# Attention scores computed as 512 cached and 64 new keys instead of two halves of 288

## The chip, the cores and the metric

The kernel runs on one core of a Trainium2 chip. The metric is the device time of one execution in microseconds (us); lower is better. Engines are called as the profile calls them: PE is TensorE's matmul side, PEld its weight loads, DVE is VectorE, ACT is ScalarE, POOL is GpSimd, SP is SyncE, which here only issues DMAs.

## The reference

The layer is a cross attention over a context of 1601 rows, a grouped-query attention and a gated feed-forward part, each added to x of 8 x 64 tokens by 512 features. The part that matters here is the second:

```python
k_sel = k_cache[block_idx].reshape(-1, NKV, HD)      # 16 blocks of 32 = 512 cached keys
k_full = jnp.concatenate([k_sel, k[0]], axis=0)      # + 64 new keys = 576
qh = q.transpose(0, 2, 1, 3)
scores = jnp.einsum('bhld,bhtd->bhlt', qh, k_full) / math.sqrt(HD)
attn = jax.nn.softmax(scores, axis=-1)
out = jnp.einsum('bhlt,bhtd->bhld', attn, v_full)
```

There are 32 query heads and 8 key heads (so 4 query heads share the keys of one group g), a head has 128 features, and there are 512 query tokens. Each head thus needs 512 x 576 scores.

## The kernel before

The program runs three stages one after the other on all engines: the cross attention (to about 290 us of the span), the grouped-query attention, called the head stage here (about 292 to 757 us), and the feed-forward part (to the end). Only the head stage is touched.

**Tiles of the head stage.** A head n (0 to 31) is the i-th of four in group g. Its 512 query tokens are four tiles qt of 128. For each tile, `score` (L1514) makes 128 x 576 scores in PSUM; DVE takes the negated row maximum (L1889), ACT the exponential with that bias and the row's sum (L1756), DVE inverts the sum (L1872), POOL scales the probabilities (L2015), PE turns them (`turn_probs`, L1540 and L1549) and multiplies them with the values (`mix`, L1558 to L1567). PE also computes the next head's queries (`queries`, L1509) and, once per group, the output projection (`output`, L1582, 48 products).

**Precision.** Every product of the stage other than the turns is made of three passes over numbers split in a high and a low part, both in the format fp32r (a 32-bit float of reduced mantissa): high x high, high x low, low x high, all added up in one PSUM bank. One matmul instruction loads 128 x 128 weights (here: the query tile, `q_t`) and then streams the moving operand (here: the keys) column by column. Each of the six products of a score tile loads its own weights, since the program issues a load for every product.

**PSUM.** A bank holds 512 numbers of 32 bits per partition. A tile of 576 scores needs two banks: 0 and 1 for even qt, 2 and 3 for odd qt. Before, each holds a half of 288 keys:

```python
for half in range(2):
    bank = 2 * (qt % 2) + half
    keys = bass.ds(g * KEYS + half * HALF, HALF)
    for step, (a, b) in enumerate(PASSES):
        mm = pe.matmul(psum[:, bank, 0:HALF], q_t[a][:, qt * P:(qt + 1) * P],
                       (k_high, k_low)[b][:, keys], start=(step == 0), stop=(step == 2))
```

**What sets the order.** It is written out by hand: `head` on PE works on qt = 0 to 3 and does, for each, a part of the next head's queries, the turn of the head before (`turn_probs`) and the score tile of this head; after the fourth come the rest of the queries and `mix` of the head before. A score tile waits until ACT has read the tile two before it (semaphore `exp`), since there are two pairs of banks. DVE and ACT wait for the last of the six products (semaphore `s`). The first DMAs of the feed-forward weights (L323) are issued by SP when the last score tile of head 31 is done. In head 30, bank 3 also holds a small sum in columns 288 to 290, which DVE reads (L1886).

Of the kernel before, what the change touches and what calls it, by code (L numbers as in the profile page):

```python
# [17 lines left out]
ALU = mybir.AluOpType  # L18
ACT = mybir.ActivationFunctionType
AX = mybir.AxisListType  # L20

P = 128
# [3 lines left out]
BATCH, SEQ, DIM = 8, 64, 512  # L26
# [25 lines left out]
NSEL = TOPK * BLOCK  # L52
ST = NSEL // P
KEYS = NSEL + SEQ

HALF = KEYS // 2
# [14 lines left out]
def wait(eng, sem, count):  # L71

    if isinstance(count, int) and count <= 0:
        return
    eng.wait_ge(sem, count)
# [1283 lines left out]
def turn_bank(qt):  # L1359

    return 4 + qt % 2


def attention_and_ffn(core, own, qo, first, xh, xl, k_high, k_low, v_sel, v_new, free):


    nc, arg, psum = core.nc, core.arg, core.psum
# [3 lines left out]
    wq_nat, wq_t, q_t = qo["wq"], qo["wq_t"], qo["q_t"]  # L1371
    wo_t = core.pack(free["wo_t"], *((f"wo_t_{s}", [P, REP, DIM], F32R) for s in ("high", "low")))
    value_high = core.sb("value_high", [P, ST + 1, HD], F32R, ctx=own)
    value_low, probs, turned_high, turned_low, mixed_high, mixed_low, piece2 = core.pack(
        free["rest"], ("value_low", [P, ST + 1, HD], F32R), ("head_probs", [P, TT, KEYS], F32),
        ("probs_t_high", [P, ST + 1, TOK], F32R), ("probs_t_low", [P, ST, TOK], F32R),
        ("mixed_t_high", [P, REP, TOK], F32R), ("mixed_t_low", [P, REP, TOK], F32R), ("w_piece2", [P, 2, PIECE], F32))
    value, probs_t, mixed_t = [value_high, value_low], [turned_high, turned_low], [mixed_high, mixed_low]
    neg_max = core.sb("neg_max", [P, TT], ctx=own)
    den = core.sb("den", [P, TT], ctx=own)  # L1380
# [8 lines left out]
    s = {k: core.sem(v, own) for k, v in names.items()}  # L1389
# [21 lines left out]
    part = core.sb("abs_part", [P, 3], ctx=own)  # L1411
# [32 lines left out]
    def gate_bank(c, k):  # L1444
        return 4 + 2 * (c % 2) + k

    def last_bank(qt):

        return (4, 5, 2, 3)[qt]

    def has_weight(g, i):

        return not isinstance(g, int) or REP * g + i < NH - 2
# [11 lines left out]
    with nc.Block() as block:  # L1465
# [37 lines left out]
        def _(pe):  # L1503
# [9 lines left out]

            def score(g, n, qt):  # L1514

                wait(pe, s["exp"], TT * n + qt - 1)
                if qt == 0:
                    pe.wait_ge(s["ql"], n + 1)
                if isinstance(g, int) and n == NH - 2 and qt == 1:
                    pe.wait_ge(s_tot, NKV)  # L1520
                    pe.matmul(psum[:, 3, HALF:HALF + 3], ones[:, :], total[:, :], start=True, stop=True).then_inc(s_all, 1)
                elif isinstance(g, int) and n == NH - 2 and qt == 3:
                    pe.wait_ge(s_co, 1)
                for half in range(2):
                    bank = 2 * (qt % 2) + half
                    keys = bass.ds(g * KEYS + half * HALF, HALF)
                    for step, (a, b) in enumerate(PASSES):
                        mm = pe.matmul(psum[:, bank, 0:HALF], q_t[a][:, qt * P:(qt + 1) * P],  # L1528
                                       (k_high, k_low)[b][:, keys], start=(step == 0), stop=(step == 2))
                mm.then_inc(s["s"], 1)  # L1530

# [171 lines left out]
        def _(act):  # L1703
# [48 lines left out]
            def exponential(n, qt):  # L1752

                act.wait_ge(s["max"], TT * n + qt + 1)
                wait(act, s["pt"], TT * (n - 1) + qt + 1)
                act.activation(probs[:, qt, :].rearrange("p (a k) -> p a k", a=2),  # L1756
                               psum[:, 2 * (qt % 2):2 * (qt % 2) + 2, 0:HALF],
                               ACT.Exp, bias=neg_max[:, qt:qt + 1], accum_out=den[:, qt:qt + 1]).then_inc(s["exp"], 1)

            def turned_high(g, i, qt):  # L1760
                act.wait_ge(s["pt"], TT * (REP * g + i - 1) + qt + 1)
# [73 lines left out]
        def _(dve):  # L1835


            def query_weight_low(g, i):
                dve.wait_ge(s["wqh"], REP * g + i + 1)
                dve.tensor_tensor(flat_wq(1), wq_nat[:, i, :], flat_wq(0), ALU.subtract).then_inc(s["wql"], 1)  # L1840

            def queries_low(i, n):
                dve.wait_ge(s["qh"], n + 1)
                dve.tensor_tensor(q_t[1][:, :], psum[:, head_bank(i), :], q_t[0][:, :], ALU.subtract).then_inc(s["ql"], 1)
# [9 lines left out]
            def mixed_low(i, n):  # L1854

                dve.wait_ge(s["ah"], n)
                dve.tensor_tensor(mixed_t[1][:, (i - 1) % REP, :], psum[:, head_bank(i), :],
                                  mixed_t[0][:, (i - 1) % REP, :], ALU.subtract).then_inc(s["al"], 1)
# [4 lines left out]
            def turned_low(g, i, qt):  # L1863
                dve.wait_ge(s["th"], TT * (REP * g + i - 1) + qt + 1)
                dve.tensor_tensor(probs_t[1][:, 0:ST, qt * P:(qt + 1) * P],  # L1865
                                  psum[:, turn_bank(qt), :].rearrange("p (t q) -> p t q", t=ST),
                                  probs_t[0][:, 0:ST, qt * P:(qt + 1) * P], ALU.subtract).then_inc(s["tl"], 1)

            def invert(n, qt):
                dve.wait_ge(s["exp"], TT * n + qt + 1)  # L1870
                wait(dve, s["norm"], TT * (n - 1) + qt + 1)
                dve.reciprocal(rden[:, qt:qt + 1], den[:, qt:qt + 1]).then_inc(s["rd"], 1)  # L1872

            def output_weight_low(g, i):
                dve.wait_ge(s["woh"], REP * g + i + 1)
                dve.tensor_tensor(wo_t[1][:, i, :], wo_nat[:, i, :], wo_t[0][:, i, :],
                                  ALU.subtract).then_inc(s["wol"], 1)

            def head(g, i, this, last, nxt):
                n = REP * g + i  # L1880
                for qt in range(TT):
                    if this:
                        dve.wait_ge(s["s"], TT * n + qt + 1)
                        if isinstance(g, int) and n == NH - 2 and qt == 1:
                            dve.wait_ge(s_all, 1)
                            dve.tensor_scalar(coeff[:, :], psum[:, 3, HALF:HALF + 3], 1.0 / WSIZE, None,  # L1886
                                              ALU.mult).then_inc(s_co, 1)
                        wait(dve, s["exp"], TT * (n - 1) + qt + 1)
                        dve.tensor_reduce(neg_max[:, qt:qt + 1],  # L1889
                                          psum[:, 2 * (qt % 2):2 * (qt % 2) + 2, 0:HALF],  # L1890
                                          AX.XY, ALU.max, negate=True).then_inc(s["max"], 1)


                    if qt > 0 and this:
                        invert(n, qt - 1)
                    if qt == TT - 1 and last:
                        tail_low(i, n)
                    elif last:
                        turned_low(g, i, qt)
                if last:  # L1900
                    turned_low(g, i, TT - 1)
                if this:
                    invert(n, TT - 1)
                if nxt:
                    queries_low(i + 1, n + 1)
                if nxt and has_weight(g, i):
                    query_weight_low(g + (i + 2) // REP, (i + 2) % REP)
                if this and i > 0:
                    if i == 1:
                        output_weight_low(g, 0)  # L1910
                    output_weight_low(g, i)
                early_weights(g, i)
                if last:
                    mixed_low(i, n)
                if this and i == 0:
                    values_low(g)
                if i == 0 and last:
                    for qt in range(TT):
                        add_output(g, qt, turn_bank(qt))

            def tail_low(i, n):

                dve.wait_ge(s["tailh"], n)
                dve.tensor_tensor(probs_t[0][SEQ:P, ST, :], psum[0:SEQ, head_bank(i), :], probs_t[0][0:SEQ, ST, :],
                                  ALU.subtract).then_inc(s["taill"], 1)

            def add_output(g, qt, bank):
                dve.wait_ge(s["o"], TT * (g - 1) + qt + 1)
                dve.tensor_tensor(core.x[:, qt, :], psum[:, bank, :],  # L1929
                                  core.x[:, qt, :], ALU.add).then_inc(s["xo"], 1)  # L1930

            def early_weights(g, i):

                if not isinstance(g, int):
                    return
                if (g, i) == (NKV - 1, 2):
                    quantise(0, 0)
                    quantise(0, 1)
                elif (g, i) == (NKV - 1, REP - 1):
                    quantise(0, 2)  # L1940
                    low(0, 0)
                    low(0, 1)
# [223 lines left out]
```

## Time and profile before

| | us |
|---|---|
| median of 3 runs | 888.73 (888.36 to 892.6) |
| the profiled execution, its own time | 887.68 |
| its span | 885.7 |
| PE busy | 845.7 (95%) |
| PEld busy | 636.2 (72%) |
| DVE busy | 609.1 (69%) |
| ACT busy | 514.3 (58%) |
| POOL busy | 459.1 (52%) |

Busy time is that in which the engine had an instruction running. The time of one matmul in the rows is from its start to its modelled end, which is longer than the distance at which the next can follow; where matmuls stand in a row, the distance between two starts is what one costs. "Idle before" and an arrow name what ended an idle time.

### The profile page before, as it was taken

To read this page: it belongs to the slowest core of one execution; us is meant where nothing else is said; L and a number is where in the kernel's file an instruction comes from. 1 tells how busy PE (TensorE), PEld (TensorE's weight loads), DVE (VectorE), ACT (ScalarE), POOL (GpSimd) and SP (SyncE) were. 2 spreads that over 40 slices of the span, in tenths; PEclk is the share of its full clock that TensorE was granted. 3 is DMA by queue.
4 is the path that set the end of the run, shared out by engine and by line. 5 is a ranking of instruction groups with operands and counts; after the bars stand their busy time and mean duration, and the time that the engine had idled before them with its cause. 6 is when DMAs were issued, how large, how long until landed. Compare 5 with 4: busy or idle time off the path is not lost.

```text
span 885.7 us, 15315 instructions
## 1 busy us (share of the span) xinstructions
PE 845.7 (95%) x5246; PEld 636.2 (72%) x5246; DVE 609.1 (69%) x1002; ACT 514.3 (58%) x989; POOL 459.1 (52%) x294
## 2 busy tenths in 40 slices
PE   6899999999999599999999999999999998899998
PEld 4444555454534488888888888888888887788886
DVE  4755677567647377586775876758758589588773
ACT  4755646464656366565665656656656577455551
POOL 2598798887661343545435444454454543334430
PEclk9899999999999899999999999999999999999999
DMA  9553443204620333060240501505105005255621
GB/s 365 196 207 122 158 176 119 84 7 117 230 107 1 131 117 122 1 214 24 72 164 0 213 24 40 193 4 205 32 5 209 13 1 180 106 174 186 210 71 48
DMA packets 42338, 102.94 MB, mean 116 GB/s; under 512 B 7859, under 2 KB 12979, under 8 KB 41395
## 3 DMA queue, kind: packets, MB, share of 16 engines
q1 hardware_dynamic: 42002, 102.06, 33.0%
q8 instruction: 29, 0.48, 0.2%
q10 hardware_dynamic: 288, 0.26, 0.1%
q14 instruction: 19, 0.15, 0.1%
HBM read 96.95 MB, written 1.05 MB: 111 GB/s over the span
## 4 chain that ended last, share of the span: by engine, by line
PE 61%; DVE 2%; POOL 1%; DMA 1%; SPq 1%; ACT 0%; issue 0%; POOLq 0%; DVEq 0%
PE psum L1528 11%; PE psum L1509 9%; PE psum L1644 9%; PE psum L1582 9%; PE psum L1540 6%; PE psum L1658 4%; PE psum L1567 3%; PE psum L1558 3%; PE psum L1563 3%; PE psum L1549 1%; DMA ffn_raw<-in_L_ffn_mean_w_dram 1%; PE psum L1559 1%; PE psum L1561 1%; SPq L323 1%; POOL head_probs L2015 0%; POOL ffn_raw L2035 0%
## 5 line engine op out<-in xcount | busy, mean ns | idle before, releaser
L2015 POOL TENSOR_TENSOR head_probs<-head_probs,inverse_den 128x576 f32<-128x576 f32 x128 | 147.5, 1153 | 203.3 <-DVE inverse_den L1872 203.3
L1201 DVE TENSOR_REDUCE max_part<-psum 128x1 f32<-128x804 f32 x128 | 121.2, 990 | 50.6 <-PE psum L753 50.2
L1065 ACT ACTIVATE probs<-psum 128x512 f32<-128x512 f32 (+1 forms) x208 | 106.8, 608 | 57.5 <-PE psum L775 56.9
L1756 ACT ACTIVATE head_probs<-psum,neg_max 128x576 f32<-128x576 f32 x128 | 94.7, 740 | 54.2 <-DVE neg_max L1889 53.5
L1889 DVE TENSOR_REDUCE neg_max<-psum 128x1 f32<-128x576 f32 x128 | 96.9, 757 | 23.3 <-PE psum L1528 22.0
L623 POOL TENSOR_TENSOR prob_sums<-prob_sums,probs 128x1024 f32<-128x1024 f32 (+1 forms) x42 | 100.2, 2385 | 7.2 <-ACT probs L1065 2.7
L1528 PE MATMUL psum<-k_high,query_t_high 128*128 (+1 forms) x256 | 87.1, 340 | 2.8 <-POOL value_low L2044 2.8
L623 POOL TENSOR_TENSOR prob_sums<-probs 128x1024 f32<-128x1024 f32 x30 | 71.3, 2381 | 33.0 <-ACT probs L1065 32.9
L1540 PE MATMUL psum<-ident,head_probs 128*128 128x128 f32 x496 | 78.9, 275 | 7.8 <-POOL head_probs L2015 6.5
L1865 DVE TENSOR_TENSOR probs_t_low<-psum,probs_t_high 128x512 fp32r<-128x512 f32 x124 | 84.7, 683 | 1.0
L2035 POOL TENSOR_TENSOR ffn_quant<-ffn_raw 128x1536 f32<-128x1536 f32 x13 | 45.6, 3512 | 68.5 <-DVE ffn_w_low L1951 26.9
L775 PE MATMUL psum<-q_t,c_t 97*128 97x512 f32 (+1 forms) x208 | 75.7, 436 | 5.4 <-ACT probs L1065 4.2
L753 PE MATMUL psum<-c_t,q_t 96*128 96x402 f32 x256 | 74.8, 375 | 4.7 <-DVE max_part L1201 4.1
L1762 ACT ACTIVATE probs_t_high<-psum 128x512 fp32r<-128x512 f32 x124 | 73.0, 588 | 6.1 <-PE psum L1549 6.1
L1528 PE MATMUL psum<-k_high,query_t_low 128*128 (+1 forms) x256 | 76.5, 299 | 0.0
L1528 PE MATMUL psum<-k_low,query_t_high 128*128 (+1 forms) x256 | 76.4, 298 | 0.0
L1540 PEld LDWEIGHTS psum<-ident,head_probs 128*128 128x128 f32 x496 | 61.4, 141 | 17.6 <-issue 10.4
L753 PEld LDWEIGHTS psum<-c_t,q_t 96*128 96x128 f32 x256 | 42.6, 188 | 42.5 <-DVE max_part L1201 28.4
L775 PEld LDWEIGHTS psum<-q_t,c_t 97*128 97x128 f32 (+1 forms) x208 | 37.1, 186 | 32.4 <-ACT probs L1065 26.9
L2027 POOL TENSOR_TENSOR w_piece<-w_piece 128x1024 f32<-128x1024 f32 x21 | 49.9, 2404 | 9.0 <-DVE value_low L1851 9.0
L1929 DVE TENSOR_TENSOR x<-psum,x 128x512 f32<-128x512 f32 x32 | 22.1, 690 | 46.9 <-PE psum L1582 46.9
L1528 PEld LDWEIGHTS psum<-k_high,query_t_high 128*128 128x128 f32 x256 | 49.3, 193 | 3.5 <-POOL value_low L2044 3.2
(242 smaller groups left out, 1903.3 us busy)
## 6 DMA issues: line engine op xcount, KB each, us to landing
ctx_t_odd<-in_ctx_dram SPq DMA_DIRECT2D x4, 3202.0 KB, 10.7
ffn_raw<-in_L_ffn_w_dram SPq DMA_DIRECT2D x42, 256.0 KB, 3.9
ffn_raw<-in_L_ffn_mean_w_dram SPq DMA_DIRECT2D x42, 256.0 KB, 4.2
w_piece<-in_L_ffn_w_dram SPq DMA_DIRECT2D x21, 512.0 KB, 6.5
w_piece<-in_L_ffn_mean_w_dram SPq DMA_DIRECT2D x21, 512.0 KB, 7.8
cache<-in_ctx_dram SPq DMA_DIRECT2D x3, 3202.0 KB, 10.5
wq_nat<-in_L_attn_wq_dram SPq DMA_DIRECT2D x32, 256.0 KB, 7.4
wo_nat<-in_L_attn_wo_dram SPq DMA_DIRECT2D x32, 256.0 KB, 3.2
```

Source lines behind the costliest of these rows:

```text
L623: pool.tensor_tensor(total[rows, :], (prob_buffer(b, t - 1) if first else total)[rows, :], prob_buffer(b, t)[rows, :], ALU.add).then_inc(s ...
L753: mm = pe.matmul(psum[:, bank + k, 0:PIECE_KEYS], q_t[0:SHIFT, b, 2 * qt:2 * qt + 2, :].rearrange("p h n -> p (h n)"), c_t[0:SHIFT, b % 3, ...
L775: pe.matmul(psum[0:rows_of(t), n % SCORE_BANKS, :], lhs, rhs[:, half * BANK:(half + 1) * BANK], start=True, stop=True).then_inc(s_sb, 1)
L1065: act.activation(prob_buffer(b, t)[0:rows, half * BANK:(half + 1) * BANK], psum[0:rows, n % SCORE_BANKS, :], ACT.Exp, scale=XSCALE).then_i ...
L1201: dve.tensor_reduce(max_part[:, qt, pair:pair + 1], psum[:, bank:bank + 2, 0:PIECE_KEYS], AX.XY, ALU.max).then_inc(s_max, 1)
L1509: mm = pe.matmul(psum[:, head_bank(i), :], wq_t[a][:, c, :], (xh, xl)[b][:, c, :], start=(k == 0), stop=(k == 3 * DC - 1))
L1528: mm = pe.matmul(psum[:, bank, 0:HALF], q_t[a][:, qt * P:(qt + 1) * P], (k_high, k_low)[b][:, keys], start=(step == 0), stop=(step == 2))
L1540: mm = pe.transpose(bank[:, t * P:(t + 1) * P], probs[:, qt, t * P:(t + 1) * P], core.ident[:, :])
L1756: act.activation(probs[:, qt, :].rearrange("p (a k) -> p a k", a=2), psum[:, 2 * (qt % 2):2 * (qt % 2) + 2, 0:HALF], ACT.Exp, bias=neg_max ...
L1865: dve.tensor_tensor(probs_t[1][:, 0:ST, qt * P:(qt + 1) * P], psum[:, turn_bank(qt), :].rearrange("p (t q) -> p t q", t=ST), probs_t[0][:, ...
L1889: dve.tensor_reduce(neg_max[:, qt:qt + 1], psum[:, 2 * (qt % 2):2 * (qt % 2) + 2, 0:HALF], AX.XY, ALU.max, negate=True).then_inc(s["max"], 1)
L2015: pool.tensor_tensor(probs[:, qt, :], probs[:, qt, :], rden[:, qt:qt + 1].to_broadcast([P, KEYS]), ALU.mult).then_inc(s["norm"], 1)
```

## The change

The six products of a score tile no longer cover 288 keys each: three cover the 512 cached keys and fill the first bank of the pair, three cover the 64 new keys and write the first 64 columns of the second. The 576 scores then lie in one piece, over the bank's edge, and DVE's maximum and ACT's exponential read them as one run of 576 in place of two runs of 288 with a gap. Nothing else changes: same products in number, same passes, same waits, same DMAs.

```diff
+    def scores_of(qt):
+        return psum[:, 2 * (qt % 2):2 * (qt % 2) + 2, :].rearrange("p a k -> p (a k)")[:, 0:KEYS]
...
-                for half in range(2):
-                    bank = 2 * (qt % 2) + half
-                    keys = bass.ds(g * KEYS + half * HALF, HALF)
+                for part, (first, count) in enumerate(((0, NSEL), (NSEL, SEQ))):
+                    bank = 2 * (qt % 2) + part
+                    keys = bass.ds(g * KEYS + first, count)
                     for step, (a, b) in enumerate(PASSES):
-                        mm = pe.matmul(psum[:, bank, 0:HALF], q_t[a][:, qt * P:(qt + 1) * P],
+                        mm = pe.matmul(psum[:, bank, 0:count], q_t[a][:, qt * P:(qt + 1) * P],
                                        (k_high, k_low)[b][:, keys], start=(step == 0), stop=(step == 2))
...
-                act.activation(probs[:, qt, :].rearrange("p (a k) -> p a k", a=2),
-                               psum[:, 2 * (qt % 2):2 * (qt % 2) + 2, 0:HALF],
-                               ACT.Exp, bias=neg_max[:, qt:qt + 1], accum_out=den[:, qt:qt + 1]).then_inc(s["exp"], 1)
+                act.activation(probs[:, qt, :], scores_of(qt), ACT.Exp, bias=neg_max[:, qt:qt + 1], accum_out=den[:, qt:qt + 1]).then_inc(s["exp"], 1)
...
                         dve.tensor_reduce(neg_max[:, qt:qt + 1],
-                                          psum[:, 2 * (qt % 2):2 * (qt % 2) + 2, 0:HALF],
-                                          AX.XY, ALU.max, negate=True).then_inc(s["max"], 1)
+                                          scores_of(qt), AX.X, ALU.max, negate=True).then_inc(s["max"], 1)
```

On PE, one turn and one score tile of head 1 (the turned probabilities `head_probs` are those of the head before; weights by moving columns) stand before as:

```order
L1540 MATMUL psum<-ident,head_probs 128x128 x4
L1549 MATMUL psum<-ident,head_probs 64x128
L1528 MATMUL psum<-k_high,query_t_high 128x288
L1528 MATMUL psum<-k_low,query_t_high 128x288
L1528 MATMUL psum<-k_high,query_t_low 128x288
L1528 MATMUL psum<-k_high,query_t_high 128x288
L1528 MATMUL psum<-k_low,query_t_high 128x288
L1528 MATMUL psum<-k_high,query_t_low 128x288
```

and at the same place with the change as:

```order
L1545 MATMUL psum<-ident,head_probs 128x128 x4
L1554 MATMUL psum<-ident,head_probs 64x128
L1533 MATMUL psum<-k_high,query_t_high 128x512
L1533 MATMUL psum<-k_low,query_t_high 128x512
L1533 MATMUL psum<-k_high,query_t_low 128x512
L1533 MATMUL psum<-k_high,query_t_high 128x64
L1533 MATMUL psum<-k_low,query_t_high 128x64
L1533 MATMUL psum<-k_high,query_t_low 128x64
```

No instruction moved on this engine or on any other, and none was added or taken away; six products have other sizes (L1528 has become L1533).

## Rows read from the trace of the kernel before

**Rows 1.** The page's table of engines: busy us, share, instructions.
```profile
PE 845.7 (95%) x5246; PEld 636.2 (72%) x5246; DVE 609.1 (69%) x1002; ACT 514.3 (58%) x989; POOL 459.1 (52%) x294
```
**Rows 2.** Busy time by stretch of the span, two stretches of the head stage.
```profile
core 0: us, PE busy (x) PEld busy (x) DVE busy (x) ACT busy (x) POOL busy (x), PEclk, DMA share, GB/s
345.00:400.00 55.00, 55.00 (x323) 48.20 (x322) 39.22 (x72) 33.65 (x72) 25.81 (x21) 1.00 0.28 97
640.00:700.00 60.00, 60.00 (x345) 52.43 (x344) 41.88 (x77) 35.85 (x75) 28.34 (x25) 1.00 0.23 83
```
**Rows 3.** The waits of PE from 290 to 757 us: total, times, longest.
```profile
PE psum L1540 <- POOL head_probs L2015: 6.5, 1, 6.5
PE psum L1528 <- POOL value_low L2044: 2.8, 1, 2.8
PE psum L1558 <- DVE probs_t_high L1924: 2.0, 2, 1.6
PE psum L1540 <- DVE probs_t_low L1865: 1.3, 2, 1.1
```
**Rows 4.** Chain that ended last, in order of time: start, length, what.
```profile
358.03 10.94 PE psum L1582 x48
...
403.16 0.44 PE psum L1540 x4
403.60 0.11 PE psum L1549
403.71 0.80 PE psum L1528 x6
...
409.27 2.08 PE psum L1509 x9
...
413.68 0.94 PE psum L1567 x4
...
697.25 10.89 PE psum L1582 x48
```
**Rows 5.** Timeline of PE, one score tile and the turn behind it: start, length.
```profile
403.68 0.30 PE L1528 MATMUL psum<-k_low,query_t_high 128*128 x1
403.81 0.30 PE L1528 MATMUL psum<-k_high,query_t_low 128*128 x1
403.94 0.30 PE L1528 MATMUL psum<-k_high,query_t_high 128*128 x1
404.08 0.29 PE L1528 MATMUL psum<-k_low,query_t_high 128*128 x1
404.21 0.29 PE L1528 MATMUL psum<-k_high,query_t_low 128*128 x1
404.34 0.60 PE L1540 MATMUL psum<-ident,head_probs 128*128 128x128 f32 x4
```
**Rows 6.** Timeline of PE, the feed-forward products of 256 columns.
```profile
764.57 0.63 PE L1644 MATMUL psum<-attn_x_low,ffn_w_high 128*128 128x256 f32 x4
765.04 0.64 PE L1644 MATMUL psum<-attn_x_high,ffn_w_low 128*128 128x256 f32 x4
```
**Rows 7.** Timeline of PEld and PE where PE resumes after idling.
```profile
752.89 0.19 PEld L1634 LDWEIGHTS psum<-wo_t_high,mixed_t_high 128*128 128x128 f32 x1 [0.91 <-DVE mixed_t_low L1967]
753.00 0.19 PEld L1634 LDWEIGHTS psum<-wo_t_low,mixed_t_high 128*128 128x128 f32 x1
753.23 0.19 PEld L1634 LDWEIGHTS psum<-wo_t_high,mixed_t_low 128*128 128x128 f32 x1
```
**Rows 8.** The page's groups of instructions: count, busy, mean ns, idle before.
```profile
L1756 ACT ACTIVATE head_probs<-psum,neg_max 128x576 f32<-128x576 f32 x128 | 94.7, 740 | 54.2 <-DVE neg_max L1889 53.5
L1889 DVE TENSOR_REDUCE neg_max<-psum 128x1 f32<-128x576 f32 x128 | 96.9, 757 | 23.3 <-PE psum L1528 22.0
```

## The prediction, made before the changed kernel was run

> **What bounds the kernel now.** I read the page's table of engines first: PE is busy for 95% of the span, the next one, DVE, for 69% [rows 1]. A share over the whole span does not say what one stage is worth, so I looked at the stage that the change touches by stretches: from 345 to 400 us and from 640 to 700 us PE has no idle time at all, at a granted clock of 1.00 (2.4 GHz), while DVE is busy for 39.2 of 55 us, ACT for 33.7 and POOL for 25.8 [rows 2]. Then I asked what PE waited for in the stage: the four waits listed come to 12.6 us in 467 us, and most of that is two waits before the stage has got going [rows 3]. Last, the chain that ended last runs through PE's own instructions without a break there, and it gives what each kind costs back to back: a score tile 0.80 us for six products (0.133 each), a turn 0.44 + 0.11 for five, nine query products 2.08, four value products 0.94, 48 output products 10.9. The output products of one group begin 339.22 us before those six groups later (358.03 and 697.25): 56.54 us for a group of four heads [rows 4].
>
> Is that time made of PE's costs alone? A group holds 16 score tiles (16 x 0.80 = 12.8), 16 turns (8.8), 48 query products (48 x 0.231 = 11.1), 56 value products (56 x 0.235 = 13.2) and 48 output products (10.9): 56.8 us against the 56.54 observed. So the head stage is a stream of products on PE, and any time added to a product there is time added to the kernel.
>
> **The change part by part.**
>
> *The large product.* 288 columns become 512, three times per tile. The trace has this size with the same format and the same weights of 128 x 128: 2.08 / 9 = 0.231 us and 0.94 / 4 = 0.235 us in the head stage, 10.89 / 48 = 0.227 in the output projection [rows 4]. I take 0.230.
>
> *The small product.* 288 columns become 64, three times per tile. No row shows an fp32r product of 64 columns, so I bound it. By columns alone: 256 columns cost 0.117 us each (0.47 us from one group of four to the next, divided by 4) [rows 6], 288 cost 0.133 [rows 5], 512 cost 0.230. These lie on a line of 0.44 ns per column plus 6 ns, which would give 64 columns 34 ns. But every product brings its own weights. Where PE starts after idling, the weight load begins at 752.89 and the next load, which can only begin when the first weights have gone into use, at 753.00: a load of 128 x 128 takes 0.11 us. The one after it is at 753.23, 0.23 later, which is the streaming time of 512 columns [rows 7]. So the cost of a product is the longer of its own stream and the load of the next weights. At 512, 288 and 256 columns the stream is longer and the load is hidden. At 64 it is not: 34 ns of stream against 110 ns of load. The turns agree: with 128 columns they stand 0.11 apart (0.44 / 4) [rows 4]. The upper bound from the nearest row is the product of 256 columns, 0.117, since a quarter of its columns should not take longer. I take 0.111 and keep 0.108 and 0.118 as ends, with 0.034 as the far lower end, which is a rival below.
>
> *A tile.* Before 6 x 0.133 = 0.798; after 3 x 0.230 + 3 x 0.111 = 1.023; 0.225 us more. Put plainly, the old split let both halves of the stream hide the weight loads; the new one stretches three products by 0.097 each and gets back only 0.022 on the other three.
>
> *How many tiles lie on the path.* There are 128 tiles [rows 8]. The four of head 0 run before PE's 6.5 us wait for POOL's first scaled probabilities [rows 3], whose cause is a DMA and a subtraction that do not depend on them, so they are hidden. The other 124 are not: 124 x 0.225 = 27.9 us. Towards the end of the stage PE waits 1.3 us for DVE's low parts and 2.0 for the tail [rows 3]; a slower PE could give DVE back about 1 us of that, which I leave in the range.
>
> *DVE and ACT.* They read 576 elements in one run in place of two. They take 757 and 740 ns and were idle before it because they waited, for PE and for each other [rows 8]; with about a quarter of both engines free in steady state [rows 2], whatever the run saves or costs is covered by the PE stream. If that cover were gone it would count 128 times, and it is not going, since PE becomes slower. I cost it at nothing. The new wait pattern is the same as before: the last of six products still releases the maximum, and it ends sooner after its start because it is short. SP's feed-forward loads are issued after the last score tile, so they move with it.
>
> The sum is made against the profiled execution: span 885.7, own time 887.68, so 915.6. The median of the runs is 1.05 us above that execution, so the predicted median is 888.73 + 27.9 = **916.6 us**. In the new trace a group should take 56.54 + 16 x 0.225 = 60.1 us.
>
> **The rivals.**
>
> *A: columns alone decide (8%).* If the load of the next weights could run ahead of the short products, for instance two loads deep, 64 columns would cost 34 ns: 3 x (230 + 34) = 792 against 798 ns, 6 ns less per tile, 0.7 us less in all: 888.0 us, no change. For it speaks that the line through 256, 288 and 512 columns is so straight. Against it speaks rows 7: loads start exactly when the weights before them go into use, never two ahead. It decides as soon as the weight load is no floor at all. The Trainium skill (TensorE: Matmul & The Clock Gate, "Back-to-back issue gap") gives this rule, N / 2.4 + 2.5 ns for N columns: 216 + 29 ns for the new pair against 2 x 122.5 for the old, which is the same 245, so by that rule the change costs nothing. Its section on LDWEIGHTS gives 128 / 1.2 = 107 ns for a load, and only both together give my sum. The same section's sustained figures, 131 ns for N=512 and 81 for N=128, would even make the new pair cheaper than the old; the trace does not agree, with 227 to 235 and 110.
>
> *B: load and stream add up in a short product (5%).* If the next load only starts after the short stream ends, the product costs 108 + 34 = 142 ns and a tile 3 x (230 + 142 - 266) = 318 ns more: 39.4 us, 928.1 us. Against it: the turns, whose load and stream are both in the same order of size, stand 0.11 apart, not 0.16 or more.
>
> *C: shorter reads on DVE and ACT matter (2%).* If one run of 576 were read quicker and the waits on these engines were what PE really waits for, the kernel could gain. But all that PE waits in the stage is 12.6 us and 9.3 of it are in the two waits at its start, which have other causes [rows 3]; 1 to 3.3 us are left, so with A at most 885 to 887 us. It would take both A and this for the kernel to become faster, and even then hardly by 0.5%.
>
> **How the numbers follow.** About 0.5% (4.4 us) is what a measurement of this kernel can tell from no change. The forecast, a load-bound small product on a PE-bound stage, has 85%. Its own range is 207 to 261 ns per tile (227 and 108, 235 and 118), so 25.7 to 32.4 us: 914.4 to 921.1. With 1 us given back by DVE waits and 1 to 2 us for the spread of the runs I make it 912 to 923. That leaves out A, B and C, some 15%. Slower by over 0.5%: the forecast, B, and what of the rest goes that way, 0.90. Same: A and part of C, 0.08. Faster: 0.02.
>
> **What would show it.** In the new profile: score products of 512 columns 0.23 us apart and those of 64 columns 0.11 apart; a score tile of about 1.02 us in the chain; 60.1 us from one group's output products to the next; PE still without idle time from 345 us on; DVE, ACT and POOL with more idle time per group and the same busy time; cross attention and feed-forward as long as before. I would be wrong if the 64-column products stood 0.03 to 0.05 apart (A) or 0.14 apart (B), or if PE showed waits in the middle of the stage, which would mean that the extra PE time displaced something else.

## The result and the profile after

| | before | with the change |
|---|---|---|
| median | 888.55 us (4 runs, 888.19 to 892.6) | 918.07 us (4 runs, 915.79 to 925.13) |
| the profiled execution, its own time | 887.68 | 916.06 |
| its span | 885.7 | 914.1 |
| ratio | | 1.034 (95%: 1.028 to 1.040) |

The kernel became slower, by 28.4 us between the two profiled executions and 29.5 us between the medians. A second set of runs, with runs of before beside it (e5 below), gave 916.30 us and 1.032 (1.028 to 1.036). The forecast was 916.6 us, with a range of 912 to 923.

The page's table of engines, with the change:

```profile
PE 874.9 (96%) x5246; PEld 649.6 (71%) x5246; DVE 607.9 (67%) x1002; ACT 517.8 (57%) x989; POOL 458.8 (50%) x294
```

PE is busy for 29.2 us more, with the same number of instructions as in [rows 1]. DVE, ACT and POOL did the same work within 4 us. The two stretches inside the head stage, to be held against [rows 2]:

```profile
core 0: us, PE busy (x) PEld busy (x) DVE busy (x) ACT busy (x) POOL busy (x), PEclk, DMA share, GB/s
345.00:400.00 55.00, 55.00 (x297) 46.64 (x297) 35.79 (x67) 32.27 (x67) 25.12 (x21) 1.00 0.27 92
640.00:700.00 60.00, 60.00 (x330) 51.04 (x329) 39.87 (x74) 35.70 (x74) 26.95 (x22) 1.00 0.26 87
```

PE still has no idle time, at the full clock; it only gets through fewer instructions in the same 55 us (297 against 323), and the other engines have fewer to do because they wait for it. The waits of PE in the stage, beside [rows 3]:

```profile
PE psum L1545 <- POOL head_probs L2017: 6.2, 1, 6.2
PE psum L1533 <- POOL value_low L2046: 2.8, 1, 2.8
PE psum L1563 <- DVE probs_t_high L1926: 2.0, 2, 1.6
...
PE psum L1545 <- DVE probs_t_low L1868: 0.8, 1, 0.8
```

The same four, 11.8 us in place of 12.6. A fifth, at the very end of the stage, grew from 0.5 to 0.7 us, so the old waits of PE took up 0.6 us of its longer work. The groups of DVE's maximum and ACT's exponential, beside [rows 8], by count, busy us, mean ns and idle before:

```profile
L1761 ACT ACTIVATE head_probs<-psum,neg_max 128x576 f32<-128x576 f32 x128 | 95.0, 742 | 72.8 <-DVE neg_max L1892 72.1
L1892 DVE TENSOR_REDUCE neg_max<-psum 128x1 f32<-128x576 f32 x128 | 96.9, 757 | 50.1 <-PE psum L1533 50.1
```

The reading in one run changed neither (757 and 742 ns against 757 and 740). DVE's wait for the scores grew from 22.0 to 50.1 us: that is where the 28 us appear on DVE.

**Where the time went.** The weight loads show it best, since a load starts when the weights before it go into use. One score tile of the new kernel on PEld (start, length), with the two instructions behind it:

```profile
402.21 0.19 PEld L1533 LDWEIGHTS psum<-k_high,query_t_high 128*128 128x128 f32 x1
402.32 0.19 PEld L1533 LDWEIGHTS psum<-k_low,query_t_high 128*128 128x128 f32 x1
402.56 0.19 PEld L1533 LDWEIGHTS psum<-k_high,query_t_low 128*128 128x128 f32 x1
402.79 0.19 PEld L1533 LDWEIGHTS psum<-k_high,query_t_high 128*128 128x128 f32 x1
403.02 0.19 PEld L1533 LDWEIGHTS psum<-k_low,query_t_high 128*128 128x128 f32 x1
403.13 0.19 PEld L1533 LDWEIGHTS psum<-k_high,query_t_low 128*128 128x128 f32 x1
403.24 0.19 PEld L1513 LDWEIGHTS psum<-attn_x_high,wq_t_high 128*128 128x128 f32 x1
403.38 0.14 PEld L1545 LDWEIGHTS psum<-ident,head_probs 128*128 128x128 f32 x1
```

From 402.32, where the first product starts to stream, the loads follow after 0.24, 0.23 and 0.23 us (512 columns each) and then after 0.11, 0.11 and 0.14 us (64 columns each). Before, six products stood 0.133 us apart [rows 5]. The six distances of this one tile add up to 1.06 us, and the query product behind it takes 0.21 in place of 0.231. What makes the last short product 0.03 longer than the other two is not known; the mean over many tiles, below, does not depend on it.

The chain that ended last shows the same tile in another light, and has the beat of the groups:

```profile
362.89 10.89 PE psum L1587 x48
...
402.38 0.11 PE psum L1554
402.49 0.95 PE psum L1533 x6
403.44 0.32 PE psum L1513
...
723.21 10.89 PE psum L1587 x48
```

The chain counts 0.95 us for the six products and not the 1.02 that was forecast. The rest stands at the instruction behind the tile: 0.32 us for one query product that otherwise costs 0.231. The chain goes by the recorded starts of the matmuls, and those of the short products and of this one lie ahead of their weights (last section). From one group's output products to the next it is (723.21 - 362.89) / 6 = 60.05 us against 56.54 [rows 4]: 21.10 us over the 96 tiles of six groups, 0.220 us for one.

Added up along the span, the 28.4 us between the two profiled executions are these:

| stretch | later or longer by |
|---|---|
| up to the first score product (294.75, then 295.84 us) | 1.1 us |
| from there to the end of PE's wait for POOL's first probabilities (308.99, then 310.83) | 0.75 |
| from there to the first output products (358.03, then 362.89), 16 tiles | 3.0 |
| six groups, 96 tiles | 21.1 |
| the rest of the program (188.5, then 190.9), 12 tiles | 2.4 |

Only the last three, 26.6 us, are the change at work; at 0.220 us a tile the 124 tiles would give 27.3, and 0.5 us of the difference is DVE's shorter wait of above. The first line is work that the change does not touch. The second holds the four tiles of head 0, and they do not set it: in the changed kernel DVE has finished all four of their reciprocals by 304.3 us, but POOL takes up the probabilities only behind a subtraction that waits for a load until 305.71. That load came 0.7 us later after the first score product than before (9.9 against 9.2 us), and this stretch scatters from 14.2 to 15.2 us over the nine traces. So 1.8 of the 28.4 us are not the price of the products, and that the sum comes out so near the forecast of 27.9 is in part luck.

### The profile page after: what moved, and what is told of

Same layout as the page of the kernel before. It is cut to its first block, busy times and chain, and to the rows that moved or that the text cites. A ratio compares the mean times of both kernels' runs of the same rounds, so it can differ in the third digit from the quotient of the medians.

```text
span 914.1 us, 15315 instructions
## 1 busy us (share of the span) xinstructions
PE 874.9 (96%) x5246; PEld 649.6 (71%) x5246; DVE 607.9 (67%) x1002; ACT 517.8 (57%) x989; POOL 458.8 (50%) x294
## 4 chain that ended last, share of the span: by engine, by line
PE 62%; DVE 2%; POOL 1%; DMA 1%; SPq 1%; ACT 0%; issue 0%; POOLq 0%; DVEq 0%
PE psum L1533 13%; PE psum L1513 10%; PE psum L1649 9%; PE psum L1587 8%; PE psum L1545 6%; PE psum L1663 4%; PE psum L1572 3%; PE psum L1563 3%; PE psum L1568 3%; PE psum L1554 1%; DMA ffn_raw<-in_L_ffn_mean_w_dram 1%; PE psum L1564 1%; PE psum L1566 1%; POOL head_probs L2017 1%; SPq L323 0%; POOL ffn_quant L2037 0%
## 5 line engine op out<-in xcount | busy, mean ns | idle before, releaser
L1892 DVE TENSOR_REDUCE neg_max<-psum 128x1 f32<-128x576 f32 x128 | 96.9, 757 | 50.1 <-PE psum L1533 50.1
L1533 PE MATMUL psum<-k_high,query_t_high 128*128 (+2 forms) x256 | 86.4, 338 | 2.8 <-POOL value_low L2046 2.8
L1533 PE MATMUL psum<-k_low,query_t_high 128*128 (+2 forms) x256 | 85.8, 335 | 0.0
L1533 PE MATMUL psum<-k_high,query_t_low 128*128 (+2 forms) x256 | 84.1, 340 | 0.0
L753 PEld LDWEIGHTS psum<-c_t,q_t 96*128 96x128 f32 x256 | 42.6, 188 | 42.5 <-DVE max_part L1201 28.4
L1545 PEld LDWEIGHTS psum<-ident,head_probs 128*128 128x128 f32 x496 | 59.5, 141 | 15.6 <-issue 7.8
L775 PEld LDWEIGHTS psum<-q_t,c_t 97*128 97x128 f32 (+1 forms) x208 | 37.1, 186 | 32.7 <-ACT probs L1065 27.7
L1533 PEld LDWEIGHTS psum<-k_high,query_t_high 128*128 128x128 f32 x256 | 49.0, 191 | 8.7 <-POOL value_low L2046 3.2
L1533 PEld LDWEIGHTS psum<-k_low,query_t_high 128*128 128x128 f32 x256 | 49.3, 192 | 6.2
```

Source lines behind the costliest of these rows:

```text
L753: mm = pe.matmul(psum[:, bank + k, 0:PIECE_KEYS], q_t[0:SHIFT, b, 2 * qt:2 * qt + 2, :].rearrange("p h n -> p (h n)"), c_t[0:SHIFT, b % 3, ...
L775: pe.matmul(psum[0:rows_of(t), n % SCORE_BANKS, :], lhs, rhs[:, half * BANK:(half + 1) * BANK], start=True, stop=True).then_inc(s_sb, 1)
L1533: mm = pe.matmul(psum[:, bank, 0:count], q_t[a][:, qt * P:(qt + 1) * P], (k_high, k_low)[b][:, keys], start=(step == 0), stop=(step == 2))
L1545: mm = pe.transpose(bank[:, t * P:(t + 1) * P], probs[:, qt, t * P:(t + 1) * P], core.ident[:, :])
L1892: dve.tensor_reduce(neg_max[:, qt:qt + 1], scores_of(qt), AX.X, ALU.max, negate=True).then_inc(s["max"], 1)
```

## The experiments

What had to be told apart: the forecast says that a product costs the longer of its own stream and the next weight load. But 64 columns in 0.11 us could as well be a slower stream for short products, or a fixed floor for any instruction, and the reading over the bank's edge was changed in the same step. Single executions of one kernel scatter by up to some 12 us (before: 886.37 to 898.55 in 21 runs), so the beat of a group of four heads, from the chain, is given beside each median; it is taken in a stretch at full granted clock (1.00 from 345 to 700 us), where the changed kernel gave 60.05 us in both of its traces.

| run | split and order | median us | ratio to before (95%) | group us | group forecast |
|---|---|---|---|---|---|
| before | 288 + 288 | 888.46 | | 56.54 | |
| e1 | 288 + 288, one run | 889.29 | 1.002 (0.999 to 1.005) | 56.54 | 56.54 |
| e2 | 336 + 240 | 889.18 | 0.999 (0.996 to 1.002) | 56.58 | 56.4 to 56.6 |
| e3 | 384 + 192 | 895.46 | 1.009 (1.006 to 1.012) | 57.45 | 57.4 |
| e7 | 448 + 128 | 904.95 | 1.018 (1.015 to 1.020) | 58.71 | 58.8 |
| e5 | 512 + 64, the change | 916.30 | 1.032 (1.028 to 1.036) | 60.05 | 60.05 |
| e6 | 512, 64 alternating | 917.95 | 1.031 (1.027 to 1.035) | 60.02 | 60.05 |
| e4 | 512 + 64, half the weights | 903.55 | 1.018 (1.013 to 1.022) | 58.45 | 58.4 |

The row of before is that of the runs beside e1 to e4; beside e5 to e7 it was 888.60 us.

### e1: the reading alone

```diff
-        return psum[:, 2 * (qt % 2):2 * (qt % 2) + 2, :].rearrange("p a k -> p (a k)")[:, 0:KEYS]
+        return psum[:, 2 * (qt % 2):2 * (qt % 2) + 2, :].rearrange("p a k -> p (a k)")[:, BANK - 288:BANK - 288 + KEYS]
...
-                for part, (first, count) in enumerate(((0, NSEL), (NSEL, SEQ))):
+                for part, (first, count, at) in enumerate(((0, 288, BANK - 288), (288, KEYS - 288, 0))):
...
-                        mm = pe.matmul(psum[:, bank, 0:count], q_t[a][:, qt * P:(qt + 1) * P],
+                        mm = pe.matmul(psum[:, bank, at:at + count], q_t[a][:, qt * P:(qt + 1) * P],
```

> Both products keep 288 columns, but the first is put at the end of its bank and the second at the start of the next, so that DVE and ACT read one run of 576 over the bank's edge: the reading part of the change alone. Theory (the cost is PE's alone: each product costs the longer of its stream and the next weight load): as before, 888.5 us within 0.3%, a group of four heads 56.54 us. Rival (the way DVE and ACT read plays a part): up to 3 us faster, or, if reading over the edge is slow and is what costs, near the changed kernel's 918 us.

Measured: 889.29 us, ratio 1.002 (0.999 to 1.005). The groups of maximum and exponential, and the beat in the chain:

```profile
L1892 DVE TENSOR_REDUCE neg_max<-psum 128x1 f32<-128x576 f32 x128 | 96.9, 757 | 23.4 <-PE psum L1533 22.1
L1761 ACT ACTIVATE head_probs<-psum,neg_max 128x576 f32<-128x576 f32 x128 | 94.7, 740 | 54.4 <-DVE neg_max L1892 53.7
```
```profile
363.30 10.89 PE psum L1587 x48
...
702.54 10.89 PE psum L1587 x48
```

Reading 576 scores in one run over the edge of a bank costs and saves nothing: 757 and 740 ns, as in two runs, and 56.54 us a group. So the whole loss belongs to the sizes of the products, and rival C is out.

### e2, e3, e7: other splits

The same edit as e1 with 336, 384 and 448 in place of 288.

> Split 336 and 240, read in one run. Theory (weight load of 0.11 us as a floor under each product): 336 columns 0.153 us, 240 columns 0.111, a tile 3 x 0.264 = 0.79 us as before, so 888.5 us within 0.5% and a group of 56.4 to 56.6 us. Rival (short products stream at a lower rate below 256 columns; 64 columns in 0.11 us would be 1.64 ns a column): 240 columns 0.40 us, a tile 0.86 us longer, about 995 us.

> Split 384 and 192, read in one run. Theory (load floor): 384 columns 0.174 us, 192 columns 0.111 instead of the 0.090 of its stream, a tile 0.057 us longer than before, 124 tiles: +7.1 us, 895.6 us, group 57.4 us. Rival (lower rate below 256 columns): 192 columns 0.32 us, about 974 us. Rival (columns alone): no change, 888.

> Split 448 and 128, read in one run. Theory (load floor): 448 columns 0.202 us, 128 columns 0.111 instead of the 0.062 of its stream, a tile 0.141 us longer than before, 124 tiles: +17.5 us, 906 us, group 58.8 us. Rival (short products stream at 1.64 ns a column): 128 columns 0.22 us, a tile 0.47 us longer, about 947 us.

Measured: 889.18, 895.46 and 904.95 us. The beats in the chain, of e2, e3 and e7 in this order:

```profile
363.57 10.89 PE psum L1587 x48
...
703.03 10.89 PE psum L1587 x48
```
```profile
358.93 10.89 PE psum L1587 x48
...
703.61 10.89 PE psum L1587 x48
```
```profile
359.74 10.89 PE psum L1587 x48
...
711.99 10.89 PE psum L1587 x48
```

Divided by six: 56.58, 57.45 and 58.71 us. One tile of e3 on PEld, for the floor itself:

```profile
450.92 0.19 PEld L1533 LDWEIGHTS psum<-k_low,query_t_high 128*128 128x128 f32 x1
451.10 0.19 PEld L1533 LDWEIGHTS psum<-k_high,query_t_low 128*128 128x128 f32 x1
451.27 0.19 PEld L1533 LDWEIGHTS psum<-k_high,query_t_high 128*128 128x128 f32 x1
451.45 0.19 PEld L1533 LDWEIGHTS psum<-k_low,query_t_high 128*128 128x128 f32 x1
451.56 0.19 PEld L1533 LDWEIGHTS psum<-k_high,query_t_low 128*128 128x128 f32 x1
451.69 0.43 PEld L1545 LDWEIGHTS psum<-ident,head_probs 128*128 128x128 f32 x4
```

384 columns take 0.18, 0.17 and 0.18 us, 192 columns take 0.11, 0.13 before the turns' load. In e7 the products of 128 columns take 0.11 and 0.13. With 192, 128 and 64 columns the short product thus costs the same 0.11 us; only the long one grows. The beats say the same more finely: with the long product taken from the line (0.44 ns a column plus 6 ns; 0.230 for 512), they leave 0.110, 0.108 and 0.109 us for a short product of 192, 128 and 64 columns. A stream of 1.64 ns per column, which would explain 64 columns as well, would have put e2 at about 995 us; it is out. With 240 columns the loss is not there yet: that is the size at which stream (0.111 by the line through 256, 288 and 512 columns) and load are equal.

### e4: the same short products, half the weights

```diff
-                        mm = pe.matmul(psum[:, bank, 0:count], q_t[a][:, qt * P:(qt + 1) * P],
+                        rows = P if part == 0 else P // 2
+                        mm = pe.matmul(psum[0:rows, bank, 0:count], q_t[a][:, qt * P:qt * P + rows],
```

> The changed kernel, but the products of the 64 new keys load only the first 64 columns of the query tile as weights; the scores of the other 64 tokens against the new keys are left out. Theory (the floor is the next weight load, which takes half as long for 64 columns): two of the three short products cost 0.058 us and not 0.11, the third is still followed by a load of 128; a tile 0.106 us shorter, 13 us faster than the changed kernel: about 903 to 905 us, group 58.4 us. Rival (a floor of 0.11 us for any product, or a slow stream for 64 columns, whatever is loaded): as the changed kernel, 916 to 918 us, group 60.05 us.

Measured: 903.55 us and, by the chain, (712.02 - 361.32) / 6 = 58.45 us a group:

```profile
361.32 10.89 PE psum L1588 x48
...
712.02 10.89 PE psum L1588 x48
```

One tile on PEld:

```profile
455.04 0.19 PEld L1534 LDWEIGHTS psum<-k_high,query_t_low 128*128 128x128 f32 x1
455.28 0.14 PEld L1534 LDWEIGHTS psum<-k_high,query_t_high 128*64 128x64 f32 x1
455.51 0.14 PEld L1534 LDWEIGHTS psum<-k_low,query_t_high 128*64 128x64 f32 x1
455.57 0.14 PEld L1534 LDWEIGHTS psum<-k_high,query_t_low 128*64 128x64 f32 x1
455.65 0.42 PEld L1546 LDWEIGHTS psum<-ident,head_probs 128*128 128x128 f32 x4
```

The two short products that run beside a load of 64 columns last 0.06 and 0.08 us (455.51 to 455.57 to 455.65), where they lasted 0.11 and 0.11; the third runs beside a load of 128 columns, as in the changed kernel. The group is 1.60 us shorter, 0.100 for a tile, so 0.05 for each of those two. By the medians the kernel is 15.1 us over before, where the changed one is 27.7 over the runs of before beside it, with the same streams. This is the run that names the weight load: an instruction floor or a slow stream would have left the time where it was.

### e5 and e6: the changed kernel again, and its products alternating

e5 is the changed kernel as it stands; this is the edit of e6.

```diff
-                for part, (first, count) in enumerate(((0, NSEL), (NSEL, SEQ))):
-                    bank = 2 * (qt % 2) + part
-                    keys = bass.ds(g * KEYS + first, count)
-                    for step, (a, b) in enumerate(PASSES):
+                for step, (a, b) in enumerate(PASSES):
+                    for part, (first, count) in enumerate(((0, NSEL), (NSEL, SEQ))):
+                        bank = 2 * (qt % 2) + part
+                        keys = bass.ds(g * KEYS + first, count)
```

> The changed kernel once more, on the chip and beside the run of before that the next two kernels share: 916 to 918 us, group 60.05 us.

> The changed kernel with its six products in the order 512, 64, 512, 64, 512, 64 in place of 512, 512, 512, 64, 64, 64. Theory (a weight load starts only when the weights before it go into use, never two ahead): each short product is still followed by a load of 0.11 us that its stream of 0.034 us does not cover, so nothing is gained: as the changed kernel within 0.5%, group 60.05 us. Rival (loads can run ahead, but three short products in a row use that up): short products cost 0.034 us, a tile 0.22 us shorter, 888 to 890 us.

Measured: 916.30 and 917.95 us. The beat of e6, then one tile of it on PEld, where a row stands for a long and a short product:

```profile
372.33 10.89 PE psum L1587 x48
...
732.46 10.89 PE psum L1587 x48
```
```profile
455.79 0.30 PEld L1533 LDWEIGHTS psum<-k_high,query_t_high 128*128 128x128 f32 x2
456.14 0.30 PEld L1533 LDWEIGHTS psum<-k_low,query_t_high 128*128 128x128 f32 x2
456.48 0.30 PEld L1533 LDWEIGHTS psum<-k_high,query_t_low 128*128 128x128 f32 x2
456.83 0.42 PEld L1545 LDWEIGHTS psum<-ident,head_probs 128*128 128x128 f32 x4
```

A pair of 512 and 64 columns costs 0.35, 0.34 and 0.35 us, that is 0.23 + 0.11, as in the other order; a group 60.02 us. A long stream of 0.23 us has room for two loads of 0.11, but the second one is not taken in advance. So order does not help, and rival A is out also where each short product has a long stream ahead of it.

The profiled execution of e6 took 924.88 us. Its head stage beats like that of e5; the time was lost ahead of it, at a granted clock of 0.94 from 20 to 290 us where the changed kernel of the first table has 0.99. That is why a difference of a few us is read here from the beat and not from a single execution.

## Why the prediction was right

- **What bounds the kernel: right.** PE was without idle time from 345 to 700 us, and what was added to its products came out in the kernel's time: 0.220 us a tile by the beat, 26.6 of the 28.4 us.
- **The long product, 0.230 us: right** (0.23 to 0.24 by the load rows).
- **The short product, 0.111 us: right, and for the reason given.** The load rows of the changed kernel show 0.11, e4 brings it to about 0.06 by halving the weights, e3 and e7 show that from 64 to 192 columns it does not depend on them. The beats give 0.108 to 0.110, at the lower end of the bounds of 0.108 and 0.118.
- **A tile, 0.225 us: 0.220 measured** by the beat; six terms, each taken to a few ns, were off by 5 ns together.
- **124 tiles on the path: right, by the trace.** They give 26.6 us against 27.9 forecast: the tile 5 ns too dear makes 0.6 of it, the shorter wait for DVE 0.5. The four tiles of head 0 are covered by a load and POOL's subtraction, as forecast. The total of 28.4 came nearer to the forecast than its parts, since 1.8 us of other origin were added.
- **What PE waits: misread in two places.** The prediction puts the 1.3 us wait for DVE's low parts towards the end of the stage; 1.1 of it lie at 315 us, near its start, and it is this one that shrank (to 0.8, with the 0.2 at the end gone). And it calls 12.6 us all that PE waits in the stage; the four waits listed are that, a fifth of 0.5 us at its end is left out. Neither changes the sum.
- **DVE and ACT at nothing: right**, by e1.
- **A score tile of 1.02 us in the chain: wrong in form.** The chain shows 0.95 us and puts the rest on the instruction behind the tile, whose own load is the one that is waited for. The beat of a group, 60.1 us forecast and 60.05 measured, is what that forecast should have been stated in alone.
- **Rivals.** A (columns alone) and B (load and stream add up, 0.142 us) are excluded by 0.11 us in the load rows and by the beat; the single 0.14 in the tile shown is not B, whose group would be 61.6 us long. C is excluded by e1. With A falls the rule of the Trainium skill (TensorE: Matmul & The Clock Gate, "Back-to-back issue gap") taken alone, by which the new pair of products costs what the old one does. The prediction's remark that sustained figures of the Trainium skill, in the same section, would make the new pair cheaper does not follow: on a straight line through its 131 ns for 512 columns and 81 ns for 128, the two pairs cost the same, some 204 ns (an estimate).

No version here beats the kernel before. e1 and e2 equal it, as they must: as long as every stream covers the load behind it, a tile is 3 x 576 columns of streaming plus 6 ns for each of six products, however it is split.

## What to carry to other kernels

In this head stage a matmul that brings its own weights costs the longer of its stream and the load of the weights behind it. So on a PE-bound stretch no part of a split moving operand should be shorter than the load: here, with 128 columns of weights and fp32r, every part wants at least some 240 columns, and 336 + 240 is as good as two equal halves. A cut at a natural boundary (full bank, cached and new keys) is paid on every short part, and neither the order of the products nor the reading in one run gives anything back. To price such a cut beforehand, take the distances between starts at several sizes, draw the line, and look for the floor where the engine resumes after idling.

One limit of the rule stands in the trace of before. In the cross attention 32 products of 33 columns in fp32, each with its own weights of 64 columns, write partitions 0 to 63 and 64 to 127 in turn:

```profile
81.18 1.01 PEld L884 LDWEIGHTS psum<-wv_u,u_all 128*64 128x64 f32 x32 [0.26 <-issue]
81.19 1.12 PE L884 MATMUL psum<-wv_u,u_all 128*64 128x33 f32 x32
```

That is 0.035 us for one, less than the 0.05 to 0.06 of e4, whose short products all write partitions 0 to 63. Products that write different partitions may overlap each other; no run here was made to try it, so the floor is shown only for products that write the same ones.

## What was not expected of the hardware

- The recorded start of a short matmul can lie ahead of its weights. In the changed kernel the products of 64 columns are recorded on PE at 403.02, 403.05 and 403.16, while their loads start at 402.79, 403.02 and 403.13:

```profile
403.02 0.19 PE L1533 MATMUL psum<-k_high,query_t_high 128*128 x1
403.05 0.27 PE L1533 MATMUL psum<-k_low,query_t_high 128*128 x1
403.16 0.28 PE L1533 MATMUL psum<-k_high,query_t_low 128*128 x1
```

  Read alone, the first distance of 0.03 us looks like rival A. For products near the floor the load rows are the ones to read.
- The floor follows the clock. Early in the head stage of the changed kernel the granted clock is 0.50 (1.2 GHz, from 310.8 to 314 us). There the same loads stand 0.42 to 0.43 us apart behind 512 columns and 0.22 behind 64, against 0.23 and 0.11 at full clock:

```profile
312.79 0.33 PEld L1533 LDWEIGHTS psum<-k_high,query_t_high 128*128 128x128 f32 x1
313.21 0.33 PEld L1533 LDWEIGHTS psum<-k_low,query_t_high 128*128 128x128 f32 x1
313.43 0.33 PEld L1533 LDWEIGHTS psum<-k_high,query_t_low 128*128 128x128 f32 x1
```
